# Score products in one run per group over shared accumulator banks, with a new order of all work

## The reference

```python
h = jnp.maximum(_layernorm(x, axis=-1), 0.0)
q = _heads(h @ Wq + bq)
k = _heads(h @ Wk + bk)
v = _heads(h @ Wv + bv)
scores = jnp.einsum('bhqd,bhkd->bhqk', q, k) / np.sqrt(HEAD_SIZE)
bias = jnp.where(graph_mask, 0.0, NEG)[:, None]
probs = jax.nn.softmax(scores + bias, axis=-1)
ctx = jnp.einsum('bhqk,bhkd->bhqd', probs, v)
x = x + (ctx.transpose(0, 2, 1, 3).reshape(x.shape) @ Wf + bf)
```

## Time and profile before

| | us |
|---|---|
| runs | 469.87, 469.96, 471.01 |
| median | 469.96 |
| span of the profiled execution, first to last instruction | 468.2 |
| median less span: what lies around the span | 1.8 |
| PE busy | 459.1 (98%) |
| DVE busy | 365.0 (78%) |
| ACT busy | 361.6 (77%) |
| POOL busy | 303.1 (65%) |

### The profile page before, as it was taken

How to read it: one execution, slowest core, us unless ns; L and a number is a source line. 1 busy time by engine, 2 the same in 40 slices (tenths; PEclk the granted TensorE clock), 3 DMA queues, 4 the chain that set the end, 5 groups by cost and what they waited for, 6 DMA issues and landing times.

```text
span 468.2 us, 12877 instructions
## 1 busy us (share of the span) xinstructions
PE 459.1 (98%) x4457; PEld 272.9 (58%) x4457; DVE 365.0 (78%) x742; ACT 361.6 (77%) x816; POOL 303.1 (65%) x308
## 2 busy tenths in 40 slices
PE   6999999999999999999999999999999999999986
PEld 2755656566575665646556575655656565555654
DVE  6989889849988695877869687687877957796855
ACT  3889999865987778877788787688877879687670
POOL 3378578683876765666857577368577648564574
PEclk9999999999999999999999999999999999999999
DMA  8156789879889796986959586969997787788797
GB/s 302 65 121 131 151 130 192 204 141 199 202 141 234 120 212 134 198 194 128 226 111 229 124 177 133 183 146 156 199 182 146 177 170 157 182 139 149 136 158 233
DMA packets 219615, 78.56 MB, mean 168 GB/s; under 512 B 199472, under 2 KB 219568, under 8 KB 219568
## 3 DMA queue, kind: packets, MB, share of 16 engines
q1 hardware_dynamic: 209200, 65.63, 71.5%
q10 hardware_dynamic: 10368, 12.33, 9.9%
HBM read 16.19 MB, written 12.58 MB: 61 GB/s over the span
## 4 chain that ended last, share of the span: by engine, by line
PE 88%; DVE 4%; DMA 3%; ACT 2%; SPq 1%; POOL 1%; issue 1%; ACTq 0%
PE ps_proj L1013 25%; PE ps_proj L1015 24%; PE ps_proj L1014 24%; PE ps_scores L1078 7%; PE ps_ctx L1013 2%; PE ps_ctx L1014 2%; PE ps_ctx L1015 2%; DMA ct_parts<-ctx_parts 1%; DMA pt_parts<-probs_parts 1%; DVE stats L822 1%; SPq L577 1%; ACT probs L757 1%; DMA x_sb<-in_x 1%; DVE w_rows L926 1%; ACT h_pairs L730 1%
## 5 line engine op out<-in xcount | busy, mean ns | idle before, releaser
L657 POOL TENSOR_TENSOR probs_parts<-probs,probs_parts 128x768 f16<-128x768 f32 x64 | 105.2, 1648 | 39.9 <-ACT probs_parts L772 39.8
L757 ACT ACTIVATE probs<-masked,neg_max 128x128 f32<-128x128 f32 x384 | 118.2, 389 | 14.4 <-DVE neg_max L885 8.2
L1015 PE MATMUL ps_proj<-ht_parts,w_lo 128*128 128x512 f16 (+1 forms) x309 | 109.6, 360 | 0.0
L1014 PE MATMUL ps_proj<-ht_parts,w_hi 128*128 128x512 f16 (+1 forms) x309 | 109.6, 360 | 0.0
L1013 PE MATMUL ps_proj<-ht_parts,w_hi 128*128 128x512 f16 (+1 forms) x309 | 109.6, 360 | 0.0
L857 DVE SCALAR_TENSOR_TENSOR qkt_lo<-ps_proj,bias_qk,qkt_hi 128x512 f16<-128x512 f32 x94 | 68.5, 742 | 27.8 <-ACT qkt_hi L741 27.8
L741 ACT ACTIVATE qkt_hi<-ps_proj,bias_qk 128x512 f16<-128x512 f32 x94 | 62.7, 679 | 34.2 <-PE ps_proj L1015 33.9
L663 POOL TENSOR_TENSOR ctx_parts<-ctx_sb,ctx_parts 128x384 f16<-128x384 f32 x62 | 56.7, 918 | 49.9 <-ACT ctx_parts L778 49.9
L876 DVE SCALAR_TENSOR_TENSOR masked<-ps_scores,score_unscale,mask 128x384 f32<-128x384 f32 x128 | 72.0, 609 | 10.3 <-PE ps_scores L1078 9.5
L642 POOL TENSOR_TENSOR h_pairs<-h_sb,h_pairs 128x384 f16<-128x384 f32 x60 | 54.3, 916 | 37.1 <-ACT h_sb L732 36.9
L652 POOL TENSOR_TENSOR x_bf<-x_sb,b_out 128x384 f32<-128x384 f32 x64 | 63.1, 1001 | 9.6 <-DVE y_sb L908 8.1
(11 more groups left out here) (113 smaller groups left out, 916.6 us busy)
## 6 DMA issues: line engine op xcount, KB each, us to landing
x_sb<-in_x ACTq DMA_DIRECT2D x56, 192.0 KB, 3.0
y<-y_sb SPq DMA_DIRECT2D x56, 192.0 KB, 2.5
x_sb<-in_x SPq DMA_DIRECT2D x8, 192.0 KB, 5.1
y<-x_bf SPq DMA_DIRECT2D x8, 192.0 KB, 3.3
pt_parts<-probs_parts SPq DMA_TRANSPOSE x64, 4.0
ct_parts<-ctx_parts SPq DMA_TRANSPOSE x62, 2.8
adj_sb<-in_adj ACTq DMA_DIRECT2D x14, 64.0 KB, 3.6
w_raw<-in_Wk SPq DMA_DIRECT2D x1, 576.0 KB, 5.1
```

The source lines that it names most:

```text
L657: nc.gpsimd.tensor_tensor(probs_parts[b][:, 1, :], probs[b % 2][:], probs_parts[b][:, 0, :], ALU.subtract).then_inc(probs_split, 1)
L757: last = nc.scalar.activation(probs[b % 2][:, u * N:(u + 1) * N], masked[b % 2][:, u, :], ACT.Exp, bias=neg_max[b % 2][:, u:u + 1])
L1014: nc.tensor.matmul(to, a_hi, b_lo, start=False, stop=False)
L1015: return nc.tensor.matmul(to, a_lo, b_hi, start=False, stop=last)
```

## The change

PSUM becomes one tensor `ps` of eight banks. Banks 0 to 5 are shared by the scores and the q/k projections; banks 6 and 7 by V, O and W, apart from a few items of single groups (`OWN_BANK`). Scores are made in three parts per group (12 pairs of matmuls each; part p writes banks p and 3 + p, the upper and the lower half of the array into different banks), and in most groups the three parts follow one another without other work between them: 20 runs in all instead of 32. `USES_BEFORE` lists, for each use of a bank, who used it before, and `free_bank` waits for that. `masked` and `neg_max` get four buffers, and the exponentials are written over the masked scores.

All turns are new, so the order changes on every engine; the number of instructions of each kind stays. The core of the diff:

```diff
 TURNS = {
-    "load": (-18036, -16566, -10822, -10793), "load_mask": (-20759,), "statistics": (-16803, -14830, -9605, -8910),
...
+    "statistics": (-29700, -29680, -19870, -19860), "aggregate": (-19850,), "additive_mask": (-19830,),
...
+    "load": (-29760, -29710, -19950, -19940), "qk_hi": (-9910, -9850, -9800, -9770, -9740, -9720),
...
+BANK = {
+    "project_qk": (0, 3, 1, 4, 2, 5), "project_v": (6, 7, 6, 7), "project_out": (6, 7, 6, 7),
+    "weigh_values": (6, 7, 6, 7),
+}
...
+SCORE_PARTS = SCORE_BANKS // HALVES
+SCORE_SLOTS = B * K // SCORE_PARTS
+LAST_PART = (0, 1, 2, 2)
...
-        masked = [sb(f"masked{n}", [P, HEADS, N]) for n in range(2)]
-        neg_max = [sb(f"neg_max{n}", [P, HEADS]) for n in range(2)]
-        probs = [sb(f"probs{n}", [P, HEADS * N]) for n in range(2)]
+        masked = [sb(f"masked{n}", [P, HEADS, N]) for n in range(B)]
+        neg_max = [sb(f"neg_max{n}", [P, HEADS]) for n in range(B)]
+        probs = [masked[n][:].rearrange("p u n -> p (u n)") for n in range(B)]
...
             def exponentials(g, b, i):
                 act.wait_ge(max_ready, nth(B, g, b, i))
-                if g >= 1 or b >= 2:
-                    act.wait_ge(probs_split, nth(B, g, b - 2, i))
...
             def mask_scores(g, b, i):
-                dve.wait_ge(scores_ready, nth(2, g, b // 2, i))
+                dve.wait_ge(scores_ready, nth(SCORE_PARTS, g, LAST_PART[b], i))
...
-                if g >= 1 or b >= 2:
-                    dve.wait_ge(probs_ready, nth(B, g, b - 2, i))
+                if g >= 1:
+                    dve.wait_ge(probs_split, nth(B, g - 1, b, i))
...
             def free_bank(stage, group, item, i):
-                before = bank_before(stage, group, item)
-                if before is not None:
-                    was, of, at = before
+                for was, of, at in USES_BEFORE[stage, group, item]:
...
+                    if was == "weigh_values":
+                        pe.wait_ge(ctx_normalized, nth(B, of, at, i))
+                    if was == "scores":
+                        pe.wait_ge(scores_masked, nth(B, of, at + 1, i))
...
-            def scores(g, pair, i):
-                if pair == 0:
+            def scores(g, part, i):
+                if part == 0:
                     pe.wait_ge(qk_split, nth(QK, g, QK - 1, i))
-                if g == 0 and pair == 0:
-                    pe.wait_ge(v_split, 1)
-                if g >= 1 or pair >= 1:
-                    pe.wait_ge(scores_masked, nth(B, g, 2 * pair - 1, i))
+                free_bank("scores", g, part, i)
...
-                for n, heads in enumerate(SCORE_PAIRS):
-                    if n == MIDDLE_BY_UPPER:
-                        pe.wait_ge(lower_done, nth(2, g, pair, i))
+                for n in range(SCORE_SLOTS):
+                    b, k = divmod(SCORE_SLOTS * part + n, K)
+                    at = slice(b * N, (b + 1) * N)
```

More of the change, by code:

```diff
@@ L51 @@
[L51 to L62, removed]
+    "scores": (0, 10, 20), "project_v": (30, 60, 70, 100), "project_out": (10130, 10140, 10200, 20040),
@@ new lines @@
+    4: {
+        "project_qk": (-150, -140, -100, -70, -60, -30), "statistics": (-580, -550, -540, -530),
+        "aggregate": (-510,), "qk_lo": (-110, -100, -90, -60, -50, -30), "shift": (-480,), "additive_mask": (-270,),
+        "qk_hi": (-250, -180, -170, -120, -110, -40), "normalize": (-440, -430, -410, -400),
+        "load": (-620, -600, -590, -540), "load_mask": (-680,), "inverse_deviation": (-290,),
+        "normed_lo": (-250, -240, -230, -220), "residual": (-100, -90, 0, 10), "transpose_normed": (-190, -180),
+    },
@@ L175 @@
+        "transpose_probs": (40, 50, 130, 160), "transpose_ctx": (120, 140, 200, 230), "store": (250, 260, 280, 330),
     },
     11: {
[L177 to L180 removed]
@@ new lines @@
+        "project_out": (-9470, -9400, -9390, -9340), "qk_lo": (-9780, -9760, -9750, -9740, -9730, -9720),
+        "values_lo": (-9620, -9580, -9490, -9480), "mask_scores": (-9690, -9680, -9650, -9610),
+        "largest_score": (-9670, -9640, -9590, -9570), "normalize_ctx": (-9420, -9330, -9270, -9140),
+        "finish": (-9160, -9070, -9040, -9000), "qk_hi": (-9870, -9860, -9850, -9840, -9790, -9760),
+        "values_hi": (-9680, -9650, -9640, -9580), "exponentials": (-9690, -9670, -9570, -9440),
@@ new lines @@
+        "statistics": (-29700, -29680, -19920, -19910), "aggregate": (-19890,),
+        "qk_lo": (-19600, -19510, -19440, -19430, -19410, -19400), "shift": (-19860,),
+        "values_lo": (-19340, -19240, -19220, -19110), "additive_mask": (-19520,),
+        "mask_scores": (-19370, -19350, -19310, -19300), "largest_score": (-19360, -19320, -19280, -19250),
+        "normalize_ctx": (-19090, -19050, -18930, -18830), "finish": (-18800, -18790, -18670, -18570),
+        "qk_hi": (-19660, -19590, -19550, -19540, -19480, -19460), "normalize": (-19900, -19880, -19800, -19770),
@@ L225 @@
-        "finish": (-28300, -28290, -28220, -28170), "store": (-29240, -29140, -29130, -29120),
+        "project_qk": (-29540, -29520, -29480, -29450, -29440, -29420),
+        "project_v": (-29330, -29320, -29270, -29260), "scores": (-29370, -29360, -29350),
+        "weigh_values": (-29210, -29170, -29050, -29040), "project_out": (-29020, -28980, -28960, -28910),
+        "statistics": (-29630, -29560, -29550, -29540), "aggregate": (-29530,),
+        "qk_lo": (-29210, -29200, -29150, -29100, -29080, -29060), "shift": (-29500,),
@@ new lines @@
+        "project_v": (-39180, -39120, -39110, -38940), "scores": (-39160, -39150, -39140),
+        "weigh_values": (-39030, -39000, -38920, -38880), "project_out": (-38900, -38850, -38830, -38790),
+        "statistics": (-39260, -39230, -39190, -39180), "aggregate": (-39170,),
+        "qk_lo": (-38840, -38820, -38760, -38750, -38740, -38730), "shift": (-39130,),
+        "values_lo": (-38710, -38630, -38590, -38350), "additive_mask": (-38880,),
+        "mask_scores": (-38700, -38680, -38650, -38640), "largest_score": (-38690, -38660, -38620, -38610),
```

476 lines of the change are left out of this document (237 added, 239 removed).

## The result

| | before | after |
|---|---|---|
| median of four runs | 469.91 us | 491.83 us |
| lowest to highest | 469.87 to 471.01 | 490.94 to 495.09 |
| span of the profiled execution | 468.2 us | 489.7 us |

A forecast was written before the change was run, and what follows sets the result against it. PE was taken as the bound, busy for 459.1 of 468.2 us, so new waits add in full. Terms -2.4 + 4.75 + 1.7 - 1.5 = +2.55 on 469.96 gave 472.5 us, range 465.9 to 476.5.

The forecast's parts named there:

- Score runs, -2.4: Scores on PE: each run costs 0.20 us beyond its pairs, so 12 runs less save 2.4 us.
- nothing is saved by joining: Rival: part boundaries cost as much as a run's ends, adding 2.4 us; chance 0.15 together with the score run's wait.
- The loop, +4.75: Groups 5 to 9: PE waits L - 2.2 us for masking behind a late load, 0.95 us in each of five groups.
- L: Time from a load's issue to its landing; 2.3 us at least, 3.1 median, 6.3 at most; taken as 3.15.
- the loads land later: Rival: a transpose beside them makes loads take 4.1 us, the loop costs 9.5, total 478.2 us; chance 0.13.
- Group 11, +1.7: W10.2 on PE waits behind group 13's late loads: chain 7.1 us against PE's 5.3; bounds 0 and 2.6.
- The start, 0: Before the loop: gains and new small waits of about the same size, counted 0, bounds -1 and +1.
- The end, -1.5: Near the end: V15.3's 1.3 us wait goes, plus 0.2 of the rest; bounds -2.1 and 0.
- The score run's wait for the last `qk_lo`: Rival: score runs wait 0.4 us if DVE is late, adding 2.4 in six groups, 474.9 us; chance 0.15 with no saving.
- The loads land in time: Rival: loop loads land within 2.3 us or leave ACT earlier, so the loop costs nothing: 466.6 us; chance 0.30.
- the first rival: The loads land in time: 466.6 us, down to 465.7 if the start gains as well; chance 0.30.

The follow-up runs named there:

- the experiment on the loads: Changed kernel with only the loads of groups 2 and 3 issued earlier on ACT: 488.30 us.
- the experiments on the loop: Changed kernel with graph 1's statistics behind the row maximum on DVE: 483.78 us; or with its load ahead of `qk_hi` of QK g.4 on ACT: 482.34 us.
- the kernels with more edits: Changed kernel with loop, group 11 and start edits together: 478.56 us; that with score runs split: 485.14; a variant with more loads earlier, `normalize` and stores moved: 479.72.
- the one with loads alone: Changed kernel with only three ACT edits, issuing the loads of the loop, of group 13 and of groups 2 and 3 earlier: 475.13 us.
- group 11 on DVE: Changed kernel with `values_lo` of V11.2 and V11.3 ahead of `aggregate` and `shift` of group 13 on DVE: 489.67 us.
- the last masking of group 0: Changed kernel with the masking of group 0's graph 3 ahead of the work of group 2 on DVE: 490.68 us.

## Why the prediction was wrong

- **Score runs, -2.4: right.** 27.97 less 27.76 us per group, 0.21 for a run, 2.5 for twelve. That nothing is saved by joining is out.
- **The loop, +4.75: the mechanism right, L mis-sized; this is one of the steps that failed.** I wrote "a transpose of normalized x will be under way beside these loads, so I take 3.15", the median of all loads. The five measured 4.15 in the mean, and the loop cost 9.4, the 9.5 of the rival "the loads land later". The rows were there to read: in the trace of before, the pair of loads at 166.72 and 167.33 went out 1.7 and 2.3 us behind such a transpose, the pair at 250.65 and 251.24 3.1 and 3.7 us behind one. (Over the whole trace of before, ten loads went out less than 2.5 us behind one: six took 4.0 to 4.9 us, four 2.4 to 3.1. The eleven that went out 2.5 to 4 us behind one took 2.3 to 3.0.) The DMA issues of these two stretches of before (KB each, median us to landing):

```profile
x_sb<-in_x ACTq DMA_DIRECT2D x2, 192.0 KB, 4.3
```

```profile
x_sb<-in_x ACTq DMA_DIRECT2D x2, 192.0 KB, 2.5
```

  After's loads of the loop go out 1.9 us behind one, with a second beside them, and where the experiment moved them ahead of both, they landed in 2.95 to 3.42. So the landing went with the company that a load had, and the median said little about it; what in that company slows a load wasn't separated. The load did not pass the `qk_hi` ahead of it: in all five groups it went out 0.2 us behind the start of that instruction, as the earlier trace rows said.
- **Group 11, +1.7: the wait right in place, half its size.** From the end of V11.2 (352.93) the second load landed after 4.3 us (4.1 said), the statistics with their hand-over took 0.8 (0.46), `aggregate` 0.46 (0.38), POOL 1.4 (1.35), `shift` 1.5 (0.2), the rest 0.7 (0.65): 9.3 instead of 7.1, against PE's 5.3 as said. The largest error is `shift`, an instruction on 4 values per partition, which I gave 0.2 us "by estimate". The trace of before had both sizes of it (first row; nanoseconds, least, median and most): 0.16 us in the median, 1.50 at most. In after (second row) the median itself is 1.11, for the reason given at the end.

```profile
L838 DVE SCALAR_TENSOR_TENSOR shift_by<-moments,rstd x15: 149/161/1502, 20.7 to 403.7; 128x4 f32<-128x4 f32 x15
```

```profile
L857 DVE SCALAR_TENSOR_TENSOR shift_by<-moments,rstd x15: 163/1111/1600, 24.8 to 418.4; 128x4 f32<-128x4 f32 x15
```

  And I counted no lower clock behind a wait (1.6).
- **The start, 0: failed.** "I found gains and new small waits of about the same size there." I had set only +-1 for it; after's profile lost 5.3. Of that, 2.1 is the wait at QK1.4 for a masking behind the late statistics of group 2: it stands, with 2.1 to 2.7, in every profile that leaves these loads and this masking where after has them, and the experiment on the loads brought it to 0.55. The 2.8 ahead of QK0.3 vary from 0.1 to 3.0 between profiles with the same order, so these runs don't show that a step of the prediction lost them.
- **The end, -1.5: about -0.3.** V15.3's wait went as said; O15.1 waits for `ct_parts`. I had named such a wait, and it lies within my bounds of -2.1 and 0, but the sum had nothing for it.
- **Other rivals.** The score run's wait for the last `qk_lo` shows once, at S11.0 (0.7 by the waits), not in six groups. "The loads land in time" is what the experiments on the loop produce there, but not in the whole kernel: no order tried came below 475.1.

The sum of what was measured, -2.5 + 9.4 + 7.4 + 5.3 - 0.3, is 19.3 of the 21.5 us. What stays open: why runs of one kernel differ by up to 6.6 us, why the kernels with more edits wait longer for `ct_parts` and `pt_parts` than the one with loads alone (which of their edits does it was not separated), and whether any such order reaches the 466.6 of the first rival.

## What to carry to other kernels

A load's landing time is read from loads in the same company (which transposes and stores are in flight), not from the median of all. When two stages come to share buffers and the work between them gets shorter, look at every instruction queued ahead of the one that frees the buffer: a load that was harmless ahead of 9.7 us of cover (where it also landed sooner) costs all that it lands late ahead of 7.1. Mend such a loss at its source, the issue of the transfer: that helped in all three places where it was tried. Moving the waiters about helped in the loop and handed the wait to the next one in two other places (group 11 on DVE, the last masking of group 0). And look at more than one profile of a kernel before a loss is put down to its order: 2.8 us of after's start were not there in other profiles with the same order.
